# Adding the second half of the attention's weighed values on the VectorE instead of by ScalarE copy and GpSimd sum

## What is computed

```python
xw  = jnp.einsum('bhtd,hde->bhte', x_h, w_att_val)
att = jnp.einsum('bhte,bhse->bhts', xw, x_h) / jnp.sqrt(d)
att = jax.nn.softmax(att, axis=-1)
vx  = x @ wv_w.T + wv_b
o   = jnp.einsum('bhts,bhsd->bhtd', att, vx)
return o @ out_w.T + out_b
```

## Time and profile before

| | |
|---|---|
| runs shown | 1566.3, 1572.76 (median), 1573.18 us |
| the profiled execution | 1568.47 us |
| its span, first to last instruction | 1566.7 us |
| attention | from about 60 to about 997 us of the span |
| feed-forward part | from about 998 us to the end |
| engine busy over the span | PE 92%, DVE 84%, ACT 55%, POOL 40% |

### The profile page before, as it was taken

The page is one execution under the profiler, slowest core; times in us unless marked ns, Lnnn a source line. Parts: engine busy times, 40 slices in busy tenths (PEclk is TensorE's granted clock), DMA queues, the critical chain, the costliest instruction groups (busy, mean ns, idle before and its releaser), DMA issues. The chain is left out here.

```text
span 1566.7 us, 32588 instructions
## 1 busy us (share of the span) xinstructions
PE 1448.9 (92%) x8554; PEld 880.3 (56%) x8554; DVE 1311.4 (84%) x2599; ACT 865.8 (55%) x1780; POOL 633.6 (40%) x868
## 2 busy tenths in 40 slices
PE   3389999999999999999999998699999999999998
PEld 2144555555555555555555554466667666666665
DVE  7588888888888888788888784499999999999995
ACT  2167677677677677767767767233333333333332
POOL 2135445355444454544535521143434334343341
PEclk8589999999999999999999999799999999999999
DMA  5644554654554456455455460000000000000000
GB/s 196 151 129 131 136 160 125 151 150 125 136 163 131 133 146 163 109 142 158 125 151 151 118 175 9 0 11 14 17 17 13 17 13 17 17 13 17 13 17 21
DMA packets 81762, 144.07 MB, mean 92 GB/s; under 512 B 19904, under 2 KB 39488, under 8 KB 81600
## 3 DMA queue, kind: packets, MB, share of 16 engines
q1 hardware_dynamic: 64992, 134.19, 30.8%
q10 hardware_dynamic: 16736, 9.46, 2.7%
HBM read 81.67 MB, written 61.93 MB: 92 GB/s over the span
## 5 line engine op out<-in xcount | busy, mean ns | idle before, releaser
L1063 DVE TENSOR_REDUCE neg_max<-ring 128x1 f32<-128x512 f32 x1024 | 636.5, 683 | 137.7 <-PE ring L840 136.6
L972 ACT ACTIVATE probs<-scores 128x512 f32<-128x512 f32 x1024 | 528.7, 604 | 208.3 <-PE scores L851 202.4
L1388 PE MATMUL gu_bank<-splits,f_x_T 128*128 128x352 f32 x1024 | 317.6, 464 | 2.1 <-ACT f_x_T L1366 2.1
L840 PE MATMUL ring<-x_stack,q_stack 64*128 64x512 f32 x1024 | 233.4, 453 | 48.9 <-DVE neg_max L1063 19.7
L867 PE MATMUL ring<-probs,v_quad 128*32 128x512 f32 x2048 | 246.2, 598 | 1.9
L1388 PEld LDWEIGHTS gu_bank<-splits,f_x_T 128*128 128x128 f32 x1024 | 191.8, 192 | 99.2 <-issue 3.2
L840 PEld LDWEIGHTS ring<-x_stack,q_stack 64*128 64x128 f32 x1024 | 98.8, 187 | 202.3 <-DVE neg_max L1063 133.3
L848 PE MATMUL scores<-q_stack,x_stack 64*128 64x512 f32 x1024 | 205.6, 395 | 2.1 <-ACT probs L972 2.1
L851 PE MATMUL scores<-max_stack,max_ones 64*128 64x512 f32 x1024 | 203.3, 391 | 0.0
L1216 POOL TENSOR_TENSOR f_rstd<-f_mean_var,eps 128x1 f32<-128x1 f32 x64 | 44.8, 699 | 331.6 <-DVE f_mean_var L1326 331.6
L715 POOL TENSOR_TENSOR pv_rows<-pv_more,pv_rows 128x512 f32<-128x512 f32 x64 | 82.0, 1281 | 198.0 <-ACT pv_more L978 198.0
(11 more groups left out here) (120 smaller groups left out, 1979.3 us busy)
## 6 DMA issues: line engine op xcount, KB each, us to landing
x_rows<-splits SPq DMA_DIRECT2D x128, 256.0 KB, 3.0
x_stack<-x_rows SPq DMA_DIRECT2D x128, 256.0 KB, 4.2
q_stack<-q_rows SPq DMA_DIRECT2D x256, 128.0 KB, 4.3
q_rows<-splits SPq DMA_DIRECT2D x64, 256.0 KB, 2.2
out_dram<-x_all SPq DMA_DIRECT2D x64, 128.0 KB, 1.7
x_all<-in_L_attn_x_dram ACTq DMA_DIRECT2D x14, 512.0 KB, 6.6
max_stack<-max_rows ACTq DMA_DIRECT2D x128, 8.0 KB
splits<-gate_up_kept SPq DMA_DIRECT2D x1, 1408.0 KB, 7.5
```

Of the source, the lines that this page charges most:

```text
L840: pe.matmul(bank(tiles[m])[:, :], row_tile(q_stack[q], m)[:, p, s * P:(s + 1) * P], row_tile(x_stack[q], m)[:, p, :], start=True, stop=Tru ...
L972: act.activation(probs[j][:, k, :], scores[k][:, :], ACT.Exp).then_inc(p_ready, 1)
L1063: dve.tensor_reduce(neg_max[g % 2][:, at:at + 1], tile[:, :], AX.X, ALU.max, negate=True).then_inc(m_used, 1)
L1388: m = pe.matmul(gu_bank[c][:, :], x_T[u][:, a, :], gate_up_T[:, a, c * CH:(c + 1) * CH], start=(a == 0), stop=(a == HALVES - 1))
```

## The change

The ScalarE's copy to `pv_more` and GpSimd's sum are taken out, with the tile `pv_more` and the semaphore `pv_ended`. The VectorE adds the bank of the second half and `pv_rows` into `pv_rows` in one instruction, in step 1, right behind the step's first `reduce_max` (that of max tile 4). The bank is now counted as empty when that sum is done (`pv_summed`). The last quad's sum is issued by the VectorE behind its loop.

```diff
-    pv_more = sb("pv_more", [P, T])
...
-        return (pv_begun, QUADS * b + g + 1) if n == 1 else (pv_ended, QUADS * b + g)
+        return (pv_begun, QUADS * b + g + 1) if n == 1 else (pv_summed, QUADS * b + g)
...
-    POOL_STEP = {(0, 0): ("maxima", "values0", "halves", "x0"), (0, 1): ("values1",), (0, 3): ("values2",),
-                 (1, 0): ("maxima", "q0", "values3"), (1, 1): ("halves", "x1"), (2, 0): ("maxima",),
-                 (2, 1): ("halves",), (2, 2): ("deviation",), (2, 3): ("q1",), (3, 0): ("maxima", "normal0"),
-                 (3, 1): ("halves", "normal1"), (3, 2): ("normal2",), (3, 3): ("normal3",)}
+    POOL_STEP = {(0, 0): ("maxima", "values0", "x0"), (0, 1): ("values1",), (0, 3): ("values2",),
+                 (1, 0): ("maxima", "q0", "values3"), (1, 1): ("x1",), (2, 0): ("maxima",),
+                 (2, 2): ("deviation",), (2, 3): ("q1",), (3, 0): ("maxima", "normal0"),
+                 (3, 1): ("normal1",), (3, 2): ("normal2",), (3, 3): ("normal3",)}
...
-            def add_halves(i, g):
-
-                pool.wait_ge(pv_begun, i + 1)
-                pool.wait_ge(pv_ended, i + 1)
-                pool.tensor_tensor(pv_rows[g % 2][:, :], pv_more[:, :], pv_rows[g % 2][:, :], ALU.add)\
-                    .then_inc(pv_summed, 1)
...
-            def end_half(i, g):
-
-                act.wait_ge(pv_done, 2 * i + 2)
-                wait(act, pv_summed, i)
-                act.activation(pv_more[:, :], bank(("pv", (g + 1) % QUADS, 0))[:, :], ACT.Copy).then_inc(pv_ended, 1)
...
-                    if j == 0 and not (first and g == 0):
-                        end_half(i - 1, (g - 1) % QUADS)
...
+            def add_halves(i, g):
+
+                dve.wait_ge(pv_done, 2 * i + 2)
+                dve.wait_ge(pv_begun, i + 1)
+                dve.tensor_tensor(pv_rows[g % 2][:, :], bank(("pv", (g + 1) % QUADS, 0))[:, :], pv_rows[g % 2][:, :],
+                                  ALU.add).then_inc(pv_summed, 1)
...
                         if ahead:
                             reduce_max(i + 2, (g + 2) % QUADS, TT * j + s)
+                        if (j, s) == (1, 0) and not (first and g == 0):
+                            add_halves(i - 1, (g - 1) % QUADS)
...
+            add_halves(LAST, QUADS - 1)
             for kind in ("rows3", "proj0", "proj1"):
                 other(kind, B)
```

More of the change, by code:

```diff
@@ L528, in attention_block @@
         sem(n) for n in ("m_ready", "m_used", "m_split", "m_low", "m_turned"))
-    s_ready, p_ready, pv_done, pv_begun, pv_ended, pv_summed = (
-        sem(n) for n in ("s_ready", "p_ready", "pv_done", "pv_begun", "pv_ended", "pv_summed"))
+    s_ready, p_ready, pv_done, pv_begun, pv_summed = (
+        sem(n) for n in ("s_ready", "p_ready", "pv_done", "pv_begun", "pv_summed"))
     misc_ready, kept_used, sum_used, recip_done = (
@@ L755, in batch @@
                                 ready_values(b, int(task[6]), first)
-                            elif task == "halves":
-                                if not (first and g == 0):
-                                    add_halves(QUADS * b + g - 1, (g - 1) % QUADS)
                             elif task == "deviation":
@@ L774, in _ @@
             batch(B - 1)
-            add_halves(LAST, QUADS - 1)
         @block.sync
@@ L1050, in _ @@
             batch(B - 1)
-            end_half(LAST, QUADS - 1)
             turn("turn0", B)
```

## The result

The changed kernel takes **1607.6 us** (median of 4 runs, 1606.5 to 1611.4) against 1569.5 for the kernel before in the same comparison: 2.5% longer, ratio 1.0248 with a 95% interval of 1.0211 to 1.0284. The forecast was 1607, range 1588 to 1626. Its profiled execution took 1606.53 us with a span of 1604.5, which is 37.8 us more than the span before.

What follows compares the result with a forecast made beforehand. TensorE was taken to bound the attention; late banks cost 39.7 us over the steps, less 2.4 at the end, sum +37.3 us. That gave 1605.8 from the profiled execution, 1610.1 from the median; forecast 1607 us, range 1588 to 1626.

Steps and rivals of the forecast that it cites:

- What bounds the kernel: Attention: TensorE, busy 57.64 of 60 us, sets the pace; busy time taken off ScalarE and GpSimd is worth nothing by itself.
- The sum's price: VectorE, behind max tile 4's reduction: each of 64 added sums takes 692 ns, with next to no idle time before it.
- The moment at which the bank comes free: Max tile 7's bank is free 1.29 us after tile 4's reduction starts; TensorE arrives after 0.72 to 0.75 and waits.
- The steps: Attention steps lose 0.65 us in (0, 1), 0.68 in (1, 1), 0.68 in (2, 1), 0.59 in (3, 1); 39.7 us in all.
- the restart of TensorE behind the wait: At max tiles 6 and 7, TensorE's matmul was taken to follow the freed bank by 0.05 us.
- This carries the forecast: Sentence saying that the moved moment at which max tile 7's bank comes free carries the forecast.
- Nothing comes back: Behind the delayed steps, TensorE's later waits move along with the delay, so none of the loss is taken back.
- The end: End of the attention: shorter sum path gives back 1.1 us at `rows1` and 1.3 at the last `rows3`, 2.4 together.
- the faster one: Rival: TensorE's 14.2 us of `rows` waits go and the sum hides in VectorE gaps; 1554 us, chance 0.07.
- the rule of the Trainium skill: Two-input elementwise work belongs on the VectorE, GpSimd being about twice as slow; by it the change is a gain.
- The rival of no change: The stall comes but is won back from TensorE's 2.36 us without a matmul in 60; 1568 to 1576 us, chance 0.06.
- the one of a delay paid twice: Rival: each quad pays at max tiles 6 and 7 and again at 8 and 9; 73 us, 1642 us, chance 0.06.

Runs made afterwards that it cites:

- the run with the bank late: Kernel before, copy and GpSimd sum kept, but the second half's bank counted as empty only when GpSimd's sum is done; 1632.2 us, ratio 1.041.
- the spare reduction: Kernel before plus one VectorE maximum over 512 SBUF constants behind the reduction of max tile 4; 1593.1 us, ratio 1.0167.
- the run with the sum first: Changed kernel with the VectorE's sum ahead of the reduction of max tile 4 instead of behind it; 1573.4 us, ratio 1.0037.
- the last experiment: Kernel before with the VectorE's direct sum in the last three quads only, and step (1, 1)'s statistics moved to (0, 2); 1561.9 us, ratio 0.9951.

## Why the prediction was right

- **What bounds the kernel**: right. No step got shorter by the 120 us of busy time that were taken off ScalarE and GpSimd.
- **The sum's price**: 680 ns against 692 taken, and no idle time before it in the steady part, as argued.
- **The moment at which the bank comes free**: right in kind and place. The wait stands at pair 6 and 7, 61 times, released by the sum, 0.53 to 0.55 us each.
- **The steps**: 0.65, 0.68, 0.68 and 0.59 were forecast for (0, 1), (1, 1), (2, 1) and (3, 1); 0.74, 0.69, 0.74 and 0.80 were measured. The term that was mis-sized is the restart of TensorE behind the wait. The prediction took 0.05 us from the freed bank to the matmul and the usual distance to the job behind it. Measured were 0.14 (533.82 to 533.96), and 0.44 instead of 0.32 to the next job. Together that is 0.2, most plainly seen in (3, 1), where nothing else is in the way. The 0.05 was read at pair 8 and 9, and there it still holds (536.02 to 536.07). At pair 6 and 7 the answer is as slow when GpSimd's sum releases it, in the run with the bank late (541.40 + 1.27 = 542.67 to 542.82, and 0.42 to the next job). So the size depends on the place and not on the engine that releases; why, no run shows.
- **"This carries the forecast"**: too simple. In three of the four steps the row of reductions alone would have cost nearly as much, as the spare reduction showed. The working by steps did contain it, as it followed tiles 5 to 8 to the next pair; the sentence did not. For the spare reduction, with its early bank, the sentence gives no loss; 1.75 us a batch were measured.
- **Nothing comes back**: right. Eleven of the sixteen steps are unchanged.
- **The end**: the 2.4 us given back were right in kind and size: 1.09 for `rows1` and 2.21 - 0.90 = 1.31 for `rows3`. But more than that came back. When the last batch starts, the changed kernel is 976.03 - 931.90 = 44.1 us behind (two starts at the same place of the timeline), and its span ends 37.8 behind. Of the difference, 2.8 come between `rows3` and the feed-forward part, and another 2.8 in the feed-forward part (1566.7 - 1004.01 = 562.7 against 1604.5 - 1044.60 = 559.9). Forecast for that start were 1.95 (three steps of the first batch) + 14 x 2.60 = 38.4, and 1.1 given back behind it (2.4 less the 1.33 of the last batch's two steps). Without the twice 2.8 us, 0.7 came back. The twice 2.8 us lie in stretches of a different granted clock (0.66 and 1.00 behind `rows3`; 0.88 and 1.00 from 12 to 26 us into the feed-forward part), for which the sum has no term. Neither is shown to be the change's own: for the first see the last section, and the feed-forward part took 563.9 us in the run with the sum first, which has the changed kernel's end, and 559.7 in the run with the bank late, which has the end of the kernel before.
- **How close the total came**: luck. The batches were put 5.7 us too cheap, nearly all of it through the restart, and 5.6 us came back with the clock in the two executions compared.
- **The rivals**: the faster one failed on the point that was named for it. With the sum ahead of the reduction the bank is free in time, and the time falls by 34 us. But even there nothing is gained over the kernel before: the waits of `rows` for GpSimd were hidden behind the VectorE's own row of work in (1, 1), so that the 0.18 won in (1, 1) was lost in (1, 2); the last experiment shortens (1, 2) with that wait left as it was. Their 14.2 us were never to be had in full. By the rule of the Trainium skill that was weighed (GPSIMD Engine Reference, "Engine selection") the VectorE was the better engine; its instruction is indeed 1.9 times as fast (680 against 1281 ns), and the kernel is slower. The rival of no change and the one of a delay paid twice both fail on the table.

## What to carry to other kernels

When work is moved onto an engine, follow the tile that waits behind it, not the engine's busy share: here the same 0.68 us cost 38 us behind one reduction and 4 us in front of it. Ask of each freed buffer when it is free and when it is wanted, and of each instruction put into a row who waits for the last of the row; each can cost most of the amount, and removing one of them then leaves much of it (here 1.75 of the 2.99 us a batch). A faster engine for a step pays where its queue is empty, which here was the last three quads of 64.

## What was not expected of the hardware

TensorE's clock at the end of the attention differs between the two profiled executions, beside a different wait for the last sum. In the kernel before, TensorE stands still for 2.21 us before the last `rows3`, and from 987 to 997 the granted clock is 0.66 on average, a mix of its two levels, 1.2 and 2.4 GHz. In the changed kernel the stand is 0.90 us, and the jobs behind it run at 1.00. The rows by stretch, first before, then after (columns as in the earlier trace rows):

```profile
987.00:997.00 10.00, 8.18 (x28) 6.26 (x28) 1.57 (x4) 1.19 (x2) 0.00 (x0) 0.66 0.00 0
```

```profile
1030.30:1040.00 9.70, 5.41 (x28) 4.21 (x28) 2.67 (x6) 1.09 (x2) 0.75 (x2) 1.00 0.00 0
```

It is tempting to say that the shorter wait kept the clock up: 1.3 us less of waiting, 2.8 us less of matmul time behind it. Two other runs speak against that. In the profiled execution of the last experiment the wait was 0.91 too, and the sixteen matmuls took 6.49 us:

```profile
985.53 0.63 PE L899 MATMUL ring<-ident,pv_rows 128*128 128x128 f32 x4 [0.91 <-DVE pv_rows L1101]
...
988.96 6.49 PE L914 MATMUL ring<-out_T,o_T 128*128 128x256 f32 x16 [0.78 <-ACT o_T L987]
```

In that of the spare reduction, which has the long wait of the kernel before, the eight and sixteen matmuls took 1.09 and 3.69:

```profile
1014.78 0.63 PE L900 MATMUL ring<-ident,pv_rows 128*128 128x128 f32 x4 [2.21 <-POOL pv_rows L716]
1016.23 1.09 PE L908 MATMUL ring<-ident,o_rows 128*128 128x128 f32 x8 [0.81 <-DVE o_rows L1105]
1018.15 3.69 PE L915 MATMUL ring<-out_T,o_T 128*128 128x256 f32 x16 [0.83 <-ACT o_T L988]
```

So either wait was seen with either speed, and the wait alone does not decide. Whether the shorter one makes the higher clock likelier, and what else decides, was not tried.
